# Copying the value accumulator out of PSUM on VectorE instead of ScalarE, in three of four transformer layers

## The reference

```python
mod = silu(c) @ w_ada + b_ada
s1, k1, g1, s2, k2, g2 = split(mod, 6)
h = layernorm(x) * (1 + k1) + s1
q, k, v = split(h @ w_qkv + b_qkv, 3)            # 16 heads of 18
p = softmax(q @ k.T * 18 ** -0.5)                # first, second, fourth layer: over 512 tokens
x = x + g1 * ((p @ v) @ w_o + b_o)
h = layernorm(x) * (1 + k2) + s2
x = x + g2 * (gelu(h @ w1 + b1) @ w2 + b2)       # first layer: two of four experts
```

## Time and profile before

| what | value |
|---|---|
| median of 3 runs | 2198.0 us (2194.46 to 2200.98) |
| the profiled execution | 2202.24 us |
| its span | 2200.5 us |
| busy TensorE / VectorE / ScalarE | 2004.8 / 1336.7 / 1142.4 us |
| copies into OS | 64, of which 48 in the first, second and fourth layer |
| mean granted TensorE clock | 0.946 |

### The profile page before, as it was taken

The page is one execution under the profiler, slowest core; times in us unless marked ns, Lnnn a source line. Parts: engine busy times, 40 slices in busy tenths (PEclk is TensorE's granted clock), DMA queues, the critical chain, the costliest instruction groups (busy, mean ns, idle before and its releaser), DMA issues.

```text
span 2200.5 us, 38987 instructions
## 1 busy us (share of the span) xinstructions
PE 2004.8 (91%) x15592; PEld 1496.7 (68%) x15592; DVE 1336.7 (61%) x2940; ACT 1142.4 (52%) x1705; POOL 208.3 (9%) x311
## 2 busy tenths in 40 slices
PE   6988999899998999999899999989997898999998
PEld 4346578748974896698575566887886646474658
DVE  4747647656674677476658482463545858684842
ACT  2353734474656365545636556554344474747463
POOL 3000111111110110011110000001100000000001
PEclk9686999899989999999999999998899999999999
DMA  5234242343234232524331412446154141314101
GB/s 160 60 120 85 74 122 63 73 122 92 77 68 136 64 86 48 152 67 100 78 104 18 131 7 65 68 78 134 30 107 111 31 114 36 96 20 112 26 3 25
DMA packets 204731, 173.97 MB, mean 79 GB/s; under 512 B 54822, under 2 KB 164678, under 8 KB 204550
## 3 DMA queue, kind: packets, MB, share of 16 engines
q1 hardware_dynamic: 197974, 158.76, 31.0%
q0 software_dynamic: 6576, 12.71, 2.1%
HBM read 125.57 MB, written 40.11 MB: 75 GB/s over the span
## 4 chain that ended last, share of the span: by engine, by line
PE 61%; DVE 20%; ACT 11%; DMA 3%; issue 3%; SPq 2%; POOL 0%; ACTq 0%; POOLq 0%; DVEq 0%
PE PSA L1890 16%; PE PSA L1905 14%; DVE MX L1529 9%; PE PSA L1680 5%; PE PSA L1794 4%; PE PSA L1771 4%; PE PSA L1741 4%; ACT PB L1378 4%; PE PSA L1784 3%; PE PSA L1753 2%; DVE HH L1659 1%; PE PSA L1814 1%; PE PSA L1703 1%; DVE FL L1429 1%; ACT FH L1408 1%
## 5 line engine op out<-in xcount | busy, mean ns | idle before, releaser
L1529 DVE TENSOR_REDUCE MX<-PSA 128x1 f32<-128x512 f32 x768 | 490.2, 682 | 292.9 <-PE PSA L1771 289.8
L1890 PE MATMUL PSA<-A,FH 128*128 128x256 f32 x2520 | 442.1, 290 | 14.0 <-DVE HH L1659 9.9
L1905 PE MATMUL PSA<-FH,HH 128*128 128x288 f32 x2016 | 443.2, 311 | 3.9 <-DVE HH L1659 3.3
L1415 ACT ACTIVATE HH<-PSA 128x512 fp32r<-128x512 f32 x252 | 150.6, 598 | 561.5 <-PE PSA L1890 552.0
L1378 ACT ACTIVATE PB<-PSA 128x1024 f32<-128x1024 f32 x384 | 370.8, 1026 | 86.4 <-PE PSA L1784 85.8
L1890 PEld LDWEIGHTS PSA<-A,FH 128*128 128x128 f32 x2520 | 362.3, 194 | 37.4 <-issue 18.7
L1905 PEld LDWEIGHTS PSA<-FH,HH 128*128 128x128 f32 x2016 | 327.1, 193 | 41.0 <-issue 32.6
L1905 PE MATMUL PSA<-FL,HH 128*128 128x288 f32 x1008 | 301.7, 299 | 0.0
L1771 PE MATMUL PSA<-KS,QS 54*128 54x512 f32 x768 | 221.4, 504 | 29.8 <-DVE MX L1529 12.2
L1283 POOL TENSOR_TENSOR X<-X,TM 128x288 f32<-128x288 f32 x128 | 101.3, 809 | 1455.2 <-DVE TM L1594 1455.2
L1659 DVE TENSOR_TENSOR HH<-PSA,HH 128x512 fp32r<-128x512 f32 x252 | 172.1, 683 | 85.1 <-ACT PSA L1416 84.5
(11 more groups left out here) (171 smaller groups left out, 2258.8 us busy)
## 6 DMA issues: line engine op xcount, KB each, us to landing
qkd<-HH SPq DMA_DIRECT2D x48, 504.0 KB
ST<-in_L_cond_w SPq DMA_DIRECT2D x51, 432.0 KB
ST<-in_L_cond_w SPq DMA_DIRECT2D x102, 192.0 KB
QS<-qkd SPq DMA_DIRECT2D x88, 144.0 KB
KS<-qkd SPq DMA_DIRECT2D x88, 144.0 KB
QS<-qkd SPq DMA_DIRECT2D x144, 72.0 KB
KS<-qkd SPq DMA_DIRECT2D x144, 72.0 KB
ST<-in_L_cond_w SPq DMA_DIRECT2D x153, 48.0 KB
```

The source lines that it names most:

```text
L1415: e.activation(r(HH[u][:, 0, :]), PS[bk][:, :], gelu)
L1529: e.reduce_max(MX[p // 2 % 2][:, col:col + 1], PS[bk][:, :], axis=AX.X).then_inc(free[bk], 1)
L1890: m = e.matmul(PS[bk][:, s_ * 256:(s_ + 1) * 256], r(w_), r(x_[:, half * 256:(half + 1) * 256]), start=(z == 0), stop=(z == 6))
L1905: m = e.matmul(PS[bk][:, 0:C], r(HH[u][:, c, tk]), r(w_), start=False, stop=(j == NCH - 1 and z == 2))
```

## The change

The step "os" is handled by ScalarE's program only in the third layer (there its copies belong to another kind of attention) and by VectorE's program in the others. The semaphores that are waited for and signalled stay the same.

```diff
@@ act_program
-                elif kind == "os":
+                elif kind == "os" and a[0] // 4 == 2:
                     i, g, (bk, n), old = a
                     if old is not None:
                         w.wait_ge(full[old[0]], old[1] + 1)
@@ dve_program
+                elif kind == "os" and a[0] // 4 != 2:
+                    i, g, (bk, n), old = a
+                    if old is not None:
+                        w.wait_ge(full[old[0]], old[1] + 1)
+                    w.wait_ge(full[bk], n + 1)
+                    e.tensor_copy(OS[:, :], PS[bk][:, :]).then_inc(free[bk], 1)
```

## The result

The changed kernel is slower: four executions took 2223.1 to 2241.4 us, median **2234.4**, against 2198.6 for before; the ratio is 1.0162, interval 1.0124 to 1.0201. Six more executions, run later, gave 2238.5 (ratio 1.0169, 1.0127 to 1.0211). The forecast was 2223, with a range up to 2231: the direction was right, the size too small.

A forecast was written before the change was run, and what follows sets the result against it. TensorE, VectorE and ScalarE were taken to bound the kernel in turns. Terms 5.1 + 11.7 + 4.4 + 1.0 + 1.1 + 1.9 = 25.2 us, on the runs' median 2198.0, gave 2223; own range 2214 to 2229, full range 2207 to 2231.

The forecast's parts named there:

- The clock: After place 2's stalls in attentions 2 and 3, TensorE's clock falls to 1.2 GHz, 0.96 us each: 1.9 us.
- place 2: Second copy of an attention (head group 1): waits for the accumulator, delaying low half, q/k write, row maxima, scores: 11.7 us.
- place 1: First copy of an attention (head group 0): lengthens VectorE's run ending in OT, for which TensorE waits: 5.1 us.
- place 4: Fourth copy of an attention (head group 3): TensorE waits for the longer copy, 1.0 us; attention 1 adds 1.1.
- place 3: Third copy of an attention (head group 2): delays the low half whose bank the maximum matmuls need: 4.4 us.
- The q/k path has slack: Rival: row maxima are late for another reason; place 2's 9.9 us and the clock's 1.9 fall away: 2211 us, chance 0.15.
- The price of the copy: A VectorE copy was taken to cost 682 ns, like a reduction of the same size, against ScalarE's 594.
- ScalarE was the bound: Rival: at 36 copies of places 1 to 3 exponentials start up to 0.59 us earlier, saving 21: 2177 us, chance 0.05.
- More knock-on: Rival: stalls of 1.7 us also lower the clock, and later L1429s make weights late: 2232 us, chance 0.10.

The follow-up runs named there:

- warm5_ve: Changed kernel, with five extra identity products on TensorE ahead of the scores at place 2 of attentions 2, 3, 7, 9, 10, 11: 2229.3 us, ratio 1.0165.
- place2: Kernel before, with VectorE making the copies only at place 2 (12 copies), ScalarE the other 36: 2212.8 us, ratio 1.0055.
- place3: Kernel before, with VectorE making the copies only at place 3 (12 copies), ScalarE the others: 2205.8 us, ratio 1.0030.
- not2: Changed kernel, with the copies at place 2 back on ScalarE, VectorE copying at places 1, 3 and 4: 2217.8 us, ratio 1.0079.
- lo_first: Changed kernel, all 48 copies on VectorE, but at places 2 and 3 behind the next q/k tile's low half: 2215.7 us, ratio 1.0061.
- rows_first_sc: Kernel before, copies on ScalarE, with SyncE issuing the row maxima's four transfers ahead of twelve q/k loads at seven places: 2229.1 us, ratio 1.0131.
- place4: Kernel before, with VectorE making the copies only at place 4 (12 copies), ScalarE the others: 2201.5 us, ratio 1.0015.
- lo_first_not1: Changed kernel, with copies at places 2 and 3 behind the q/k tile's low half and those at place 1 on ScalarE: 2202.9 us, ratio 1.0021.
- not1: Changed kernel, with the copies at place 1 back on ScalarE, VectorE copying at places 2, 3 and 4: 2230.1 us, ratio 1.0150.
- place1_again: Second run of the kernel before with VectorE making the copies only at place 1, ScalarE the others: 2212.1 us, ratio 1.0046.
- before_again: Kernel before, unedited, timed against itself, giving its second trace: 2199.7 us, ratio 1.0000.

## Why the prediction was wrong, and where it was right

The direction, the path and the waits were right. The step that failed is *The clock*: "I count both, 1.9". It should have been 11 to 13: 11.5 by the clock of the executions, 12.5 by the table below. The forecast had two falls at 0.96 us each, behind the two longest stalls of place 2. The two traces of the changed kernel have seven and nine that before has not, at some 1.4 us: at place 1, where the forecast looked for none, behind stalls of place 2 that it left out, and in attention 6.

To see it by place, take for each attention the time from the start of the last value matmul of one group to that of the next, and compare the second traces: the changed kernel (2237.8 us, near its median) with before (2204.2), and warm5_ve with the same. Attention 1 counts at place 4 alone. Longer by, in us, with the number of stretches in which the lower level shows in either trace (the forecast's column is without its 1.9 for the clock):

| place | forecast | changed | falls | warm5_ve | falls |
|---|---|---|---|---|---|
| 1 | 5.1 | 10.7 | 4 | 9.5 | 3 |
| 2 | 11.7 | 15.0 | 6 | 12.0 | 1 |
| 3 | 4.4 | 8.3 | 6 | 4.9 | 1 |
| 4, with attention 1 | 2.1 | 1.8 | 0 | 1.8 | 0 |
| sum | 23.3 | 35.8 | | 28.2 | |

The six falls at place 2 and the six at place 3 are the same ones: they last across the border, so only the sum of the two places, 23.3 us, is firm. Attention 4's stands in the trace of before too. Where the others are taken away, these places cost what was forecast, 12.0 and 4.9 for 11.7 and 4.4. So the waits of the sum were right to half a us for each place.

The two whole spans differ by 33.6 us, 2.2 less than the sum. Attention 1 is 4.1 us shorter at its places 1 to 3, where before's trace is at the lower level for 10 us and the changed kernel's not at all; that varies from trace to trace (10 us in place2, none in place3). What is left of the kernel is 1.9 longer.

The profiled execution of 2223.1 us shows where its luck lay. At the same places it is 35.4 us longer than before's second trace, as much as the slower one; it is the rest of the kernel, attention 1 with it, that was 16.4 us shorter, with less time at the lower level. So it agrees with the forecast in the total alone. At places 1 to 3 of attentions 2 to 12 the two traces of the changed kernel stand 34 and 38 us at the lower level, those of before 3.4 each; the difference of the medians' clocks, 0.007, would be some 31 us of it (0.007 x 2200 / 0.5, an estimate).

- *Place 1.* Where the clock does not fall, the stretch is 0.6 us longer, as forecast; attention 11 has 0.4 (0.5 forecast), attention 9 was -0.3 as forecast. Where it falls it is 2.0 to 2.1. The wait for OT itself grew by less than 0.6 (0.83 to 0.98 in attention 3); the rest stands ahead of it, at the maximum matmuls. The forecast looked for falls behind place 2 alone and had none here. Place 1 alone costs 13 to 20 us, not 5.1.
- *Place 2.* Confirmed by three edits: the wait appears with place2 (18.8 us) and goes with not2 (9.3) and nearly with lo_first (10.7). The rival "The q/k path has slack" is refuted twice, by place2 and by rows_first_sc.
- *Place 3.* 0.6 in most attentions, as forecast, and 4.9 us in the run of place 3 alone. With place 2 before it, up to 2.8 (attention 6): the clock.
- *Place 4.* 0.05 to 0.06 each and 1.2 in attention 1 (0.09 and 1.1 forecast).
- *The price of the copy.* 687 ns for 682. The Trainium skill (VectorE: DVE Perf Modes, "Why PSUM operands drop a tier") has fp32 from PSUM at 1x, an estimate of 658 ns, and the trace agrees better with that than with the up to 2x of the tier table, an estimate of 392 ns.
- *ScalarE was the bound.* Refuted: the wait for exponentials fell by 3.2 us between the first traces and by 0.8 between the second ones, not by 21. The Trainium skill (ScalarE: Activation LUTs, "Rules for kernel authors") puts relu, max, min, add and mul on VectorE, with its speed in bf16 as the reason. It does not name a copy: carrying it over to an fp32 copy out of PSUM was the prediction's own step, and that does not hold here. At this size the copy takes 687 ns there and 594 on ScalarE, and what stands behind it in VectorE's queue matters more than either.
- *More knock-on* (2232, 0.10) was the nearest: stalls of 1.7 us did lower the clock. It still fell short: four more falls of 0.96 are 3.8 us, where one costs 1.4 at place 1 and, in attention 6, 2.2 at place 3, and it had none at place 1. Its other half, weights that come late, shows little: TensorE's wait for FL (L1429) went from 7.5 us to 8.0.

Why was the size of a fall wrong? It was read as the difference of two stretches of the same matmuls, but the one without a fall, attention 3's, was not undisturbed. The fall in attention 4 of before, and two starts of attention 3's scores there:

```profile
690.41:693.83 3.42, 3.42 (x22) 1.07 (x14) 3.36 (x7) 3.29 (x5) 0.00 (x0) 0.50 0.41 135
```

```profile
478.13 0.50 PE L1784 MATMUL PSA<-QS,KS 56*128 56x512 f32 x2 [0.20 <-ACT PB L1378]
...
482.38 1.13 PE L1784 MATMUL PSA<-QS,KS 56*128 56x512 f32 x4
```

From the scores after the stall, two rounds of matmuls take 4.38 us when nothing holds them (the third round of attention 3, 480.48 to 482.38, twice, and 0.58 for the transposes). Attention 3 took 4.94 (475.54 to 480.48), as one pair of its scores waited for exponentials; attention 4 took 5.91 (688.95 to 694.86). Against 4.38 its fall costs 1.5, not 0.96. Like against like, the matmuls of attention 3 after the stall say the same: 3.39 us at 0.52 in the changed kernel and 1.89 at full clock in warm5_ve. The Trainium skill (TensorE: Matmul & The Clock Gate, "Terms") puts the penalty at the throttled time times the share of the clock that is missing, an estimate of 1.6 here (3.39 x 0.48); the rows agree.

That the clock falls because TensorE stands still is shown for place 2 by warm5_ve. For place 1 it is argued from the traces alone. The falls come right behind its waits, one to four in each trace with its copies on VectorE. With them on ScalarE the traces of before, place2, place3, place4 and lo_first_not1 show none there; not1 shows one, in attention 9, and rows_first_sc one, in attention 10, so a fall at place 1 does not need the copy. No run kept TensorE busy in that wait.

## What to carry to other kernels

Moving a wait to another engine's queue moves it in front of everything behind it there: before moving an instruction, ask what stands behind it and whether that is ready earlier, and put the waiting one behind it (here worth 21 of 37 us). When stalls of TensorE grow, price the matmuls after them at the lower clock as well, and look for such falls behind short waits too: here 11 to 13 us on top of some 24. A forecast against a median needs the clock of typical executions; the profiled one was the fastest of ten.

## What was not expected of the hardware

- In attention 5, place 1, TensorE did the same matmuls and stood still 1.51 us among them (place1_again) or 1.07 (before_again), each time with 0.97 at the end. After the first the clock was at the lower level, and seven matmuls took 3.3 us; after the second it was not, and they took 1.9.
- The executions of one kernel differ by their clock, 0.943 to 0.957 in before, at 1.64 us per 0.001; 94 of them lie within 2188 to 2213 us; ten of the changed kernel already take in 2223 to 2250.
- Falls behind place 3 hardly come from place 3 itself (alone: 0.950, 4.9 us); most come where the longer stall of place 2 lies just ahead. Attentions 4 and 6 show falls at places 2 and 3 even with the copies there on ScalarE (both traces of place 1 alone).
- Twelve loads and four small transfers in one queue of SyncE: loads first, the scores wait 8.5 us for the maxima; maxima first, the maximum matmuls wait 22.5 us for the loads, and the kernel is 29 us slower.
